# A language-model tower kernel: the second span's rule groups three a step from step 2 on, the first of the three between score tile and value products

## What is computed

```python
rule_matrices = rule_transform[token_rules[token_ids]]
h = einsum('bsd,bsde->bse', base_embeddings[token_ids], rule_matrices)
h = h + attn(layernorm(h))   # softmax(q k / 8) x, then VO
h = h + ffn(layernorm(h))    # top 2 of 8 experts, relu, W1, W2
```

## Time and profile before

| | |
|---|---|
| unprofiled runs | 619.15, 620.26 and 611.41 us; median 619.15 |
| profiled execution | 610.8 us, of which 608.8 us from first to last instruction |
| PE busy | 495.7 us, 81% of the span |
| DVE, ACT, POOL busy | 411.8, 287.2, 229.1 us |
| mean granted TensorE clock | 0.93 of full |
| chain of work that ended last | PE 55%, DVE 18%, POOL 9%, issue 8% |

### The profile page before, as it was taken

The page is one execution under the profiler, slowest core; times in us unless marked ns, Lnnn a source line. Parts: engine busy times, 40 slices in busy tenths (PEclk is TensorE's granted clock), DMA queues, the critical chain, the costliest instruction groups (busy, mean ns, idle before and its releaser), DMA issues.

```text
span 608.8 us, 9495 instructions
## 1 busy us (share of the span) xinstructions
PE 495.7 (81%) x2764; PEld 270.0 (44%) x2764; DVE 411.8 (68%) x1003; ACT 287.2 (47%) x581; POOL 229.1 (38%) x375
## 2 busy tenths in 40 slices
PE   0168404878777888999999999999999999999985
PEld 0036302444442334445544544554454445576663
DVE  5634288883126756888868968986984876755477
ACT  0205101037663535465565565555566545547673
POOL 5765356462425200431352254032322313181542
PEclk9999665579998997999999999999999999999988
DMA  8825210919620171532330431134042200000000
GB/s 237 316 65 168 62 35 28 210 57 232 195 79 18 35 171 36 123 74 63 82 76 2 104 90 34 30 90 101 2 104 63 52 2 11 1 10 2 11 2 17
DMA packets 21792, 47.05 MB, mean 77 GB/s; under 512 B 6249, under 2 KB 11577, under 8 KB 21681
## 3 DMA queue, kind: packets, MB, share of 16 engines
q1 hardware_dynamic: 15408, 32.23, 21.9%
q0 software_dynamic: 4752, 8.20, 4.5%
q10 hardware_dynamic: 1584, 6.03, 3.0%
HBM read 9.97 MB, written 11.01 MB: 34 GB/s over the span
## 4 chain that ended last, share of the span: by engine, by line
PE 55%; DVE 18%; POOL 9%; issue 8%; DMA 4%; ACT 4%; SPq 2%; DVEq 0%; ACTq 0%; POOLq 0%
PE bank L1304 15%; PE bank L1290 10%; PE bank L1266 7%; POOL ctxT L522 5%; PE bank L1214 4%; PE bank L1236 4%; DVE mx L1009 4%; DMA ctxT<-in_table,ids 2%; PE bank L1208 2%; PE bank L1209 2%; DVE r_sb L1067 2%; POOL r_sb L595 2%; POOL emb_sorted L532 1%; PE bank L1315 1%; PE bank L1249 1%
## 5 line engine op out<-in xcount | busy, mean ns | idle before, releaser
L1009 DVE TENSOR_REDUCE mx<-bank 128x1 f32<-128x512 f32 x256 | 170.7, 687 | 79.0 <-PE bank L1290 72.8
L595 POOL TENSOR_TENSOR r_sb<-r_sb 128x256 f32<-128x256 f32 x174 | 90.9, 523 | 248.9 <-DVE r_sb L1085 168.5
L675 ACT ACTIVATE prob<-bank 128x512 f32<-128x512 f32 x256 | 138.8, 597 | 68.7 <-PE bank L1266 56.3
L1304 PE MATMUL bank<-prob,xa 128*64 128x512 f32 x448 | 123.5, 630 | 0.0
L1290 PE MATMUL bank<-ks,qs 96*128 96x512 f32 x240 | 111.4, 467 | 13.9 <-DVE mx L1009 13.8
L1290 PEld LDWEIGHTS bank<-ks,qs 96*128 96x128 f32 x240 | 46.2, 193 | 121.8 <-issue 103.4
L1266 PE MATMUL bank<-qs,ks 97*128 97x512 f32 x224 | 77.3, 427 | 0.0
L742 ACT ACTIVATE r_sb<-bank,stay 128x512 f32<-128x512 f32 x56 | 37.1, 687 | 44.9 <-PE bank L1209 44.6
L1266 PEld LDWEIGHTS bank<-qs,ks 97*128 97x128 f32 x224 | 38.6, 194 | 15.3 <-issue 10.5
L522 POOL DMA_INDIRECT ctxT<-in_table,ids x32 | 33.2, 1036 | 22.5 <-DMA ctxT<-in_table,ids 9.6
L532 POOL DMA_INDIRECT emb_sorted<-ctxT,pos x32 | 32.3, 1009 | 20.4 <-DMA emb_sorted<-ctxT,pos 12.2
(11 more groups left out here) (173 smaller groups left out, 696.2 us busy)
## 6 DMA issues: line engine op xcount, KB each, us to landing
qs<-qk_h SPq DMA_DIRECT2D x64, 128.0 KB, 2.5
ks<-qk_h SPq DMA_DIRECT2D x56, 128.0 KB, 2.5
qs<-qk_l SPq DMA_DIRECT2D x32, 128.0 KB, 2.5
ks<-qk_l SPq DMA_DIRECT2D x28, 128.0 KB, 2.4
emb_sorted<-front ACTq DMA_DIRECT2D x4, 608.0 KB, 9.7
y_sorted<-y_out POOLq DMA_DIRECT2D x19, 128.0 KB, 2.4
e_in<-emb_sorted POOLq DMA_DIRECT2D x9, 256.0 KB, 4.0
emb_sorted<-front ACTq DMA_DIRECT2D x3, 640.0 KB, 9.7
```

The costliest lines, as they stand in the source:

```text
L595: nc.gpsimd.tensor_tensor(a[:, at:at + width], src[:, 0:width], src[:, width:2 * width], ALU.add).then_inc(S["pool_chain"], 1)
L675: nc.scalar.activation(prob[:, step % NPROB, u % 2, :], bank[u % NST][:], ACT.Exp, scale=SC).then_inc(S["exp_done"], 1)
L1009: V.tensor_reduce(mx[:, u // 16, at_:at_ + 1], score_bank(n)[:], AX.X, ALU.max).then_inc(S["mx_done"], 1)
L1304: last = M(bank[5][64 * hh:64 * hh + 64, :], xa[:, b % XAR, ut, :], prob[:, step, hh, :], start=(ut == 0), stop=(ut == J - 1))
```

## The change

`R_AT` puts three entries in a step, from step 2 on, where it put four in a step, from step 3 on; the last two entries are in step 8 instead of step 7. `aux_at` lists the first two actions of a step's groups ahead of the other actions. The new function `lead` returns these two; PE does them after the first score tile and before the value products, and ACT does its share of them before the copy of bank 5.

```diff
-        R_AT = [(0, 3 + g // 4) for g in range(20)]
+        R_AT = [(0, 2 + g // 3) for g in range(20)]
...
+            return groups[0:2] + todo + groups[2:]
+
+        def lead(b, k):
+
+            return [a for a in aux_at(b, k)[0:2] if a[0] in ("rT", "rule")]
...
-                    for a in aux_at(b, k):
+                    for n_, a in enumerate(aux_at(b, k) + [("", 0, 0)]):
+                        if n_ == len(lead(b, k)) and k % 4 == 3 and 0 <= b < LAST:
...
                     score_tile()
+                    for a in lead(b, k):
+                        aux(a)
...
-                    for a in aux_at(b, k):
+                    for a in aux_at(b, k)[len(lead(b, k)):]:
```

More of the change, by code:

```diff
@@ L259, in aux_at @@
             todo = []
+            groups = [a for g in range(TOTAL - BASE[1] + 1) if R_AT[g] == (b, k)
+                      for a in ([("rT", BASE[1] + g, 0)] if g < NG[1] else []) + ([("rule", BASE[1] + g - 1, 0)] if g else [])]
             if b == LAST:
@@ L682, in _ @@
                         nc.scalar.copy(ctxT[:, b % 2, pair, th * HW:(th + 1) * HW], summed(n)[:, 0:HW]).then_inc(S["ctx_copied"], 1)
[L683 to L689, removed]
-                    for a in aux_at(b, k):
+                    for n_, a in enumerate(aux_at(b, k) + [("", 0, 0)]):
+                        if n_ == len(lead(b, k)) and k % 4 == 3 and 0 <= b < LAST:
+                            pair = k // 4
+                            act.wait_ge(S["pv_done"], 16 * b + k + 1)
+                            if b >= 2:
+                                act.wait_ge(S["vo_ps"], J * (b - 1))
+                                act.wait_ge(S["srow_in"], 32 * (b - 1))
+                            nc.scalar.copy(ctxT[:, b % 2, pair, :], bank[5][:]).then_inc(S["ctx_copied"], 1)
                         kind, ab, i = a
```

## The result

| | before | after |
|---|---|---|
| median of 20 runs each | 614.59 us (609.1 to 625.63) | 608.88 us (605.45 to 611.45, but for two of 613.4 and 613.9 and one of 673.9) |
| ratio, 95% interval | | 0.9933 (0.9906 to 0.9961) |
| profiled execution (its span) | 610.8 us (608.8) | 610.1 us (608.0) |

The ratio compares the runs that lie within 1.5% of the fastest run of their kernel, 14 of 20 before and 19 of 20 after. It is 4.1 us (2.4 to 5.8) in the 613.3 us that those 14 have in the mean; the two medians are 5.7 us apart. The direction is the forecast one, and the size about twice the 2.1 us that I had. The forecast of 617.0 stood on a median of three runs, 619.15; with twenty it is 614.59. The two profiled executions differ by 0.7 us only, so a single pair of spans would have misled: the profile has to be read by stretches.

What follows compares the result with a forecast made beforehand. The last rule group leaving PSUM was taken to set PE's step 12. Waits falling from 10.7 to 6.5 us, less 2.15 for an extra step, save 2.1: 617.0 us, own range 615.9 to 618.2, 8 in 10 607.5 to 621.

Steps and rivals of the forecast that it cites:

- One step more: Groups in steps 2 to 8 put a seventh plain step in the phase: last group 2.15 us later, called certain.
- The leading pair's cover costs nothing: Steps 3 to 8: value products and a score tile cover the leading group's `eT` copies; wait costed at nothing.
- The leads' loads: Register loads of leading groups, steps 4 to 8: 0.6, 0.3 and three times 0.15 us, together 1.4 us.
- The third group: Third group still waits once a step: 0.3 in step 3, 1.0 in 4 and 5, 0.75 in 6 and 7; 3.8 us.
- Step 2: Transpositions wait for DVE's two projection read-outs, 0.6 us, and for the first `y_out` copy, 0.35 us: 0.95 us.
- The sum: Waits fall from 10.7 to 6.5 us, less 2.15 for the extra step: last group leaves 2.1 us earlier.
- All behind step 12 keeps its distance: Step 12 begins 2.1 us earlier, and everything behind it keeps the same order and distances.
- The clock rival: Longer idle ahead of step 12 lengthens PE's low clock into steps 14 and 15, costing 2.2 us: 619.2 us; chance 0.18.
- The second sign of being wrong: The forecast is wrong if the stretch from 190 to 210 us, around step 12 and after, is longer than before.
- The rival that leads aren't hidden: Each lead pays 0.35 us plus its whole load: 4.1 us instead of 1.4, time 619.8 us; chance 0.17.
- More hidden than I sum: Waits in the group phase of 4.6 us instead of 6.5: 4.0 us earlier, 615.1 us; chance 0.15.
- The level, 617.0: Whole kernel's unprofiled median: 619.15, which is 8.35 above the profiled time, shifted by 2.1 us to 617.0 us.

Runs made afterwards that it cites:

- e12: Changed kernel with its table one step later, three groups a step from step 3 on, ending in step 9; 612.79 us (12 runs), ratio 0.9966.
- e2: Changed kernel without the lead place: new table kept, all three entries a step behind the value products; 614.39 us (12 runs), ratio 1.0003.
- e3: The changed kernel run and profiled again, nothing altered; 609.33 us (9 runs), ratio 0.9926.
- e5: Changed kernel with seven unused multiplications of constants on PE behind step 11's work, filling the wait for step 12; 609.26 us (10 runs), ratio 0.9926.
- e6: Changed kernel with the layer norm of sequence 2 in step 12 instead of 11; 604.83 us (4 runs), ratio 0.9863.
- e9: Changed kernel with sequence 2's layer norm one step later and four unused multiplications behind step 12's work on PE; 605.33 us (6 runs), ratio 0.9868.
- e7: The kernel before run and profiled again, nothing altered; one run, 614.0 us.
- e11: Kernel before with only the layer norm of sequence 2 one step later; 610.84 us (11 runs), ratio 0.9939.
- e8: Changed kernel with four groups a step instead of three, from step 2 on; 608.16 us (6 runs), ratio 0.9914.
- e1: Changed kernel with the old table, four groups a step from step 3 on, lead place kept; 611.07 us (12 runs), ratio 0.9964.
- e10: Lead place with four groups a step from step 3 on, and sequence 2's layer norm one step later; 607.67 us (6 runs), ratio 0.9884.

## Why the prediction was right, point by point

- **What bounds (right).** The chain of last copy, store, gathers, norm, maximum and step 12 is in the profiles of both kernels. Its length was 12.77 us in the profile at hand, 11.8 in the three others of the two kernels.
- **One step more, 2.15 us (right).** e12: 1.4 us, which is 2.15 less the 0.8 us that step 2's waits give back.
- **The leading pair's cover costs nothing (right).** No bracket at the second group in any quiet step; e2, without it, has the bracket back (0.59).
- **The leads' loads, 1.4 us (right in the two profiles of the changed kernel, too high in others).** 0.90 by the bracket in step 4, about 0.1 in each of the others; 1.4 together. But that load was 1569 ns, above my bound of 1045, and e3 has one of 1563. In e5, e6 and e9 it is 1044, 801 and 678 ns, and the leads wait 0.5 to 0.8 us together. My own sign of being wrong, a bracket of 0.7 us and more at a lead, did show: once, in step 4, in both profiles. It was that one load and not the wait behind each lead that the rival meant.
- **The third group, 3.8 us (right, a little high).** Intervals 1.21, 2.38, 1.61, 1.59 and 1.59 us, 3.5 over the 0.98 of work. I had a mean of 1.59 and 1.88 for the quiet steps; it was 1.59 each time. The four other profiles of this phase have 3.1 to 3.8.
- **Step 2, 0.95 us (size right in four of five profiles).** It holds three transpositions and two products, 2.15 + 3 x 0.32 + 2 x 0.66 = 4.43 us of work. It took 5.28 us in e3, e5, e6 and e9, so 0.85 of waits, and 5.94 in the first profile after, so 1.5. There it was the groups' data that was late, which I had excluded. PE's and POOL's timelines of the kernel after:

```profile
138.10 0.63 PE L1137 MATMUL bank<-cst,e_in 128*128 128x128 f32 x4 [1.31 <-DMA e_in<-emb_sorted]
```

```profile
134.71 2.93 POOL L402 DMA_DIRECT2D e_in<-emb_sorted  x4 [1.95 <-DMA emb_sorted<-ctxT,pos]
```

  POOL issued the loads 0.95 us later than in rows 6, while step 2 began 0.78 us earlier, and the groups now ask 3.4 us sooner in the step. In e9 the data was late too (0.54). In e3 it was DVE's read-outs (0.23 and 0.16), as written.
- **The sum, 2.1 us at the last group (too small; this is the step that failed).** On the first pair of profiles it is 2.64 us from step 2 on, which is 5.9 us of waits against my 6.5: that far the sum held. With the second pair it is 5.0 (43.73 to 38.70), and by three executions of the one phase and five of the other 4.8. Two terms were off. The waits before, 10.7 us, were those of one execution: e7 has 11.7 and e11 11.9, both with the lower clock in the phase. And the waits after, 6.5 us, are 5.9, 4.5, 4.0, 4.0 and 4.3, in the mean 4.5. Of the 2.0 us between, 0.4 are the leads' loads and 0.4 the third groups' intervals. Most of the rest is a saving that the sum didn't have: ahead of the value products a product gives way after 0.51 us (167.33 to 167.84) where I counted 0.66, and step 3, at 5.15 us, takes 0.17 us less than its work and waits counted that way. Waits of 10.7 and 6.5 give 2.1; waits of 11.4 and 4.5 give the 4.8.
- **All behind step 12 keeps its distance (not in the profiles, about right over the runs).** In the first pair 3.5 of 4.4 us were gone by copy 1. The clock rival, at 0.18, described this execution: the lower clock reached into step 14, which it named, though not into step 15. And its price of 2.2 us is near the 2 us that the filled wait of e5 took away. The second sign of being wrong was in it: from step 12 to copy 0 it took 13.4 us (e3 12.7) where it had taken 11.6. But the kernel before has that too in e7 (13.7), and over the runs the changed kernel is faster all the same, which the rival excluded.
- **The rival that leads aren't hidden** fell with the brackets of steps 6 to 8, where the leads have loads and show none. **More hidden than I sum**, waits of 4.6 and 4.0 us at 0.15, is nearest to what the ratio and the five profiles show.
- **The level, 617.0.** 8.35 us of offset were taken from three runs. Twenty give an offset of 3.8 us for the kernel before (614.59 to 610.8), and -1.2 for the one after (608.88 to 610.1), so the profiled executions lie on different sides. The measured 608.88 is 8.1 us below 617.0 and outside the forecast's own range of 615.9 to 618.2. Of the 8.1, 4.6 are the median of three runs, and 3.6 are the change, which is 5.7 us by the medians where I had 2.1. That 608.88 lies inside the wide range, 1.4 us from its lower end, is owed to the spread that I had added for the runs, not to the sum. The direction and the mechanism were forecast; that the number held was in good part luck.

## What to carry to other kernels

When two engines hand short pieces to each other, put one piece where the other engine's answer has other work over it; one such place a step was worth 6 us of a 43 us phase here, while spreading the pieces without it gave nothing that could be measured in the time. Ask then what the phase's end releases: moving the consumer of that chain one step later (a table entry) was worth about as much again as the change, by the medians. And take the terms of a sum from at least two executions where they hold waits, since here a register load, a gather and the clock each moved a stretch by 1 us from one execution to the next.

## What the runs showed of the hardware

- The granted clock also fell inside the group phase: from 163 to 166 us in e7 and from 152.5 to 159.5 in e11, with no wait of PE over 1.0 us in the 10 us ahead, and from 157 to 163 in e8, there behind a wait of 1.58 us. All three have four groups a step (PE busy for 6.24 of 8.28 us in a quiet step); the first profile of before, e1 and e10 have four a step too, and it didn't fall, nor did it in the eight profiles with three a step. Why it falls in some executions isn't shown.
- Register loads of four numbers by PE's sequencer: 328 ns at the least, but 1569 and 1563 ns for the first one of the phase in two executions of the changed kernel, in steps where the DMA share was 0.95 and 0.99; in e5, e6 and e9 the same load took 1044, 801 and 678 ns. A median over 18 hides this.

```profile
L1127 PEldq TENSOR_LOAD <-trow x18: 328/464/1569, 56.5 to 172.0; - x18
```

- A wait of 5.1 us on PE cost 2 us more behind its end, by the clock, and seven unused multiplications in it took these away in their place (e5, clock 1.00 where e3 has 0.58). The whole wasn't measurably faster for it.
